# Router's sum over edges: the second one-hot of each step is made by TensorE transposes and a ScalarE copy instead of a VectorE comparison

## The reference, cut to what matters

```python
e = leaky_relu(a_src[src] + a_dst[dst], negative_slope=0.2)
e_max = segment_max(e, dst, num_segments=M)
ee = exp(e - e_max[dst])
denom = segment_sum(ee, dst, num_segments=M)
alpha = ee / (denom[dst] + 1e-16)
msg = h[src] * alpha[:, :, None]
agg = segment_sum(msg, dst, num_segments=M)
```

## Time and profile before

| | |
|---|---|
| median of three runs | 7634.4 us |
| the profiled execution, its own time | 7647.61 us |
| its span | 7645.7 us |
| busy, share of the span | PE 68%, PEld 54%, DVE 70%, ACT 34%, POOL 65% |
| mean granted TensorE clock | 0.75 of full speed |
| first and last `near_hot` of the router's sum | 7077.7 and 7475.6 us |
| first and last start of `add_up` | 7089.1 and 7493.1 us |

### The profile page before, as it was taken

One profiled execution on the slowest core, in us unless ns is written; L12 is line 12 of the kernel. 1 busy time (PEld: TensorE's weight loads), 2 busy tenths in 40 slices (PEclk: granted clock), 3 DMA queues, 4 the chain that ended last, 5 costly groups with the idle time before them and its releaser, 6 DMA issues. The chain is left out here.

```text
span 7645.7 us, 108407 instructions
## 1 busy us (share of the span) xinstructions
PE 5222.5 (68%) x27325; PEld 4150.9 (54%) x27325; DVE 5368.0 (70%) x15063; ACT 2576.8 (34%) x8277; POOL 4995.8 (65%) x5420
## 2 busy tenths in 40 slices
PE   6988766666666666566666666666669999998440
PEld 3655445555555555446556566556546666665340
DVE  8989746555555555667777777777757777777997
ACT  0000034444444444344444444444322222222220
POOL 2432317777777777557777777777247777776991
PEclk7555597878778778787878887887668888887555
DMA  1000234444444444344444444444333222322437
GB/s 32 4 8 4 47 103 134 135 134 135 133 135 133 133 134 135 107 122 131 131 130 131 131 131 131 131 131 131 113 62 63 59 62 59 63 58 55 126 92 181
DMA packets 504047, 777.31 MB, mean 102 GB/s; under 512 B 121545, under 2 KB 364222, under 8 KB 503442
## 3 DMA queue, kind: packets, MB, share of 16 engines
q0 software_dynamic: 202656, 454.22, 22.6%
q1 hardware_dynamic: 292838, 304.95, 15.0%
q10 hardware_dynamic: 7948, 11.21, 0.6%
HBM read 698.60 MB, written 71.36 MB: 101 GB/s over the span
## 5 line engine op out<-in xcount | busy, mean ns | idle before, releaser
L695 POOL DMA_INDIRECT att_kv_e<-kv,gnn_idx x3336 | 3195.4, 958 | 1193.6 <-issue 978.9
L771 PE MATMUL att_ps_sum<-att_vals,att_hot 128*125 128x136 f32 x6672 | 1301.7, 353 | 1537.9 <-DVE att_vals L825 1537.2
L771 PEld LDWEIGHTS att_ps_sum<-att_vals,att_hot 128*125 128x125 f32 x6672 | 1098.6, 239 | 1744.2 <-DVE att_vals L825 1735.9
L806 DVE TENSOR_TENSOR att_prod<-att_ps_q,att_kv_e 128x512 f32<-128x512 f32 x834 | 576.2, 691 | 1314.6 <-DMA att_kv_e<-kv,gnn_idx 797.1
L695 POOL DMA_INDIRECT max_rows<-rows,gat_idx x1128 | 1068.2, 947 | 564.8 <-issue 336.4
L758 PE MATMUL att_ps_q<-qs,att_hot_t 125*128 x6672 | 1195.9, 339 | 27.4 <-DVE att_hot_t L813 27.4
L758 PEld LDWEIGHTS att_ps_q<-qs,att_hot_t 125*128 125x128 f32 x6672 | 1142.5, 256 | 28.6 <-issue 28.6
L789 ACT ACTIVATE att_hot<-node_no,gnn_loc 128x125 f32<-128x125 f32 x3336 | 1044.3, 384 | 8.2 <-PEq L85 8.2
L1859 DVE CUSTOM_DVE_ANT_0 max_junk<-max_far,max_ps_b 125x256 bf16<-125x256 bf16 x2256 | 793.0, 416 | 259.4 <-PE max_ps_b L1823 258.4
L782 ACT ACTIVATE att_ps_dve<-att_clipped 128x32 f32<-128x32 f32 x834 | 167.7, 201 | 2310.9 <-DVE att_clipped L833 2310.5
L841 DVE TENSOR_TENSOR acc<-acc,att_ps_sum 125x136 f32 x1668 | 486.3, 292 | 125.2 <-DVE acc L841 12.0
(11 more groups left out here) (447 smaller groups left out, 7492.3 us busy)
## 6 DMA issues: line engine op xcount, KB each, us to landing
att_local<-gnn_loc_rows SPq DMA_DIRECT2D x834, 128.0 KB
att_kv_e<-kv,gnn_idx POOLq DMA_INDIRECT x3336, 3.0
max_local<-gat_loc_rows SPq DMA_DIRECT2D x282, 128.0 KB
gs_local<-gat_loc_rows SPq DMA_DIRECT2D x141, 256.0 KB, 3.2
outs<-ex_y SPq DMA_DIRECT2D x25, 896.0 KB
max_rows<-rows,gat_idx POOLq DMA_INDIRECT x1128, 2.4
ans_late<-outs SPq DMA_DIRECT2D x11, 896.0 KB
ans_early<-outs SPq DMA_DIRECT2D x8, 896.0 KB
```

Of the source, the lines that this page charges most:

```text
L695: pool.indirect_dma_start(rows(j, e), None, source, bass.IndirectOffsetOnAxis(ap=g.idx[:, t:t + 1], axis=0))\
L771: ins = pe.matmul(ps_sum[j % 2][0:NODE_TILE, p * 256:p * 256 + SUMS], hot[:, j, PAIR * p + e, :], vals[:, j % 2, PAIR * p + e, :], start=e ...
L806: dve.tensor_tensor(prod[:].rearrange("p (e d) -> p e d", e=GROUP), ps_q[j % 2][:, :].rearrange("p (e d) -> p e d", e=GROUP), kv_e[:, j, : ...
```

## The change

`one_hot` goes from VectorE, and `node_no` and its filling with it. In its place TensorE gets a piece `turn_hots` with lag -1 at the end of its list: eight transposes of `hot_t` (each 125 by 128, by way of the identity) into one of two PSUM tiles `ps_hot`, after `fetch` of two steps later. ScalarE gets a piece `copy_hots` with lag -2 at the end of its list, which copies 1000 columns from PSUM into `hot`. `hot_t` now has four buffers, and `near_hot` waits for the transposes of four steps earlier instead of the fetch of two steps earlier.

```diff
-        node_no = sb("node_no", [LANES, WIDE, NODE_TILE], BF16)
-        hot_t = sb("hot_t", [NODE_TILE, 2, WIDE * LANES], BF16)
+        hot_t = sb("hot_t", [NODE_TILE, 4, WIDE * LANES], BF16)
+        ps_hot = [st.enter_context(nc.psum_tensor(f"gs_ps_hot{h}", [LANES, 1024], BF16)) for h in range(2)]
...
-                                        hot_t[:, j % 2, e * LANES:(e + 1) * LANES],
+                                        hot_t[:, k % 4, e * LANES:(e + 1) * LANES],
...
+            def turn_hots(k, r, j):
+                wait(pe, m["one_hots"], k - 1)
+                for e in range(WIDE):
+                    ins = pe.transpose(ps_hot[j % 2][:, e * LANES:e * LANES + NODE_TILE],
+                                       hot_t[:, k % 4, e * LANES:(e + 1) * LANES], c.ident16[0:NODE_TILE, 0:NODE_TILE])
+                ins.then_inc(m["turned"], 1)
...
-            steps(pe, [(1, load_tiles), (-5, add_up), (1, fetch)])
+            steps(pe, [(1, load_tiles), (-5, add_up), (1, fetch), (-1, turn_hots)])
...
-            steps(act, [(-3, high), (-4, middle), (-1, exps)])
+            def copy_hots(k, r, j):
+                act.wait_ge(m["turned"], k + 1)
+                wait(act, m["summed"], (k - 4) + 1)
+                act.copy(hot[:, k % 4], ps_hot[j % 2][:].rearrange("p (e n) -> p e n", e=WIDE)[:, :, 0:NODE_TILE])\
+                    .then_inc(m["one_hots"], 1)
+            steps(act, [(-3, high), (-4, middle), (-1, exps), (-2, copy_hots)])
...
-            dve.memset(acc3[:], 0.0)
-            chain(dve.tensor_copy(node_no[:], c.node_no[:, 0:1, :].broadcast_to([LANES, WIDE, NODE_TILE])))
+            chain(dve.memset(acc3[:], 0.0))
...
-            def one_hot(k, r, j):
-                wait(dve, m["summed"], (k - 4) + 1)
-                dve.tensor_tensor(hot[:, k % 4], node_no[:], g.loc[:, bass.ds(k * WIDE, WIDE)].unsqueeze(2)
-                                  .broadcast_to([LANES, WIDE, NODE_TILE]), ALU.is_equal).then_inc(m["one_hots"], 1)
...
-                wait(dve, m["fetched"], k - 1)
-                dve.tensor_scalar(hot_t[:, j % 2, :], local[0:NODE_TILE, j], c.lane_no[0:NODE_TILE, :], None, ALU.is_equal)\
+                wait(dve, m["turned"], (k - 4) + 1)
+                dve.tensor_scalar(hot_t[:, k % 4, :], local[0:NODE_TILE, j], c.lane_no[0:NODE_TILE, :], None, ALU.is_equal)\
...
             steps(dve, [(0, gather_info), (-6, add_sum(0)), (-1, leaky), (-6, add_sum(1)), (2, near_hot), (-6, add_sum(2)),
-                        (-2, one_hot), (-6, add_sum(3)), (-6, load_tiles)])
+                        (-6, add_sum(3)), (-6, load_tiles)])
```

More of the change, by code:

```diff
@@ L1937, in neighbour_sum @@
         ps_n, ps_sum = psum("ps_n"), psum("ps_sum")
-        m = sem_set(nc, st, "gs", ["tiles_in", "cleared", "one_hots", "near_hots", "fetched", "info", "sums", "leaky",
+        ps_hot = [st.enter_context(nc.psum_tensor(f"gs_ps_hot{h}", [LANES, 1024], BF16)) for h in range(2)]
+        m = sem_set(nc, st, "gs", ["tiles_in", "cleared", "turned", "one_hots", "near_hots", "fetched", "info", "sums", "leaky",
                                    "less", "exps", "weighted", "high", "rest", "middle", "split", "summed", "added",
```

## The result

The changed kernel takes 7553.3 us (median of four runs, 7550.7 to 7561.8) where the kernel before takes 7634.1: a ratio of 0.9897, 95% interval 0.9879 to 0.9914, or 81 us less. The prediction was 7528 us in a range of 7495 to 7573. So the direction and the range hold, and of the 106 us forecast a quarter is missing; the time lies 3 us above the 7506 to 7550 to which the prediction gave 60%. The profiled execution takes 7550.7 us with a span of 7548.8.

The account below looks back on a forecast made before the run. VectorE and GpSimd were taken as the bound, fully busy at 2.905 us a step. VectorE's 2.10 plus 0.05 gives 2.15; 136 steps save 103 us, the ends 4, so 7528 us, range 7495 to 7573.

Parts of the forecast that it names:

- VectorE's 2.10 us: VectorE's time per step of the router's sum: 2.91 us, less the comparison's 1.11, plus 0.30 for the exposed add wait.
- their 0.43: On VectorE, the third and fourth add, now adjacent, would start 0.43 us apart, since one waits for the other.
- the 0.05 for handovers: Added to VectorE's 2.10 us because four engines hand work to each other, making 2.15 us a step.
- One of the prediction's own signs of being wrong: Signs: ScalarE's copy over 1.3 us, transposes over 0.15 us apart, or a step paced by a wait it did not name.
- the costly handovers: Rival, 18%: VectorE's waits for GpSimd or unhidden TensorE weight loads give 2.45 us a step, 7569 us.
- the 0.89 forecast: TensorE's eight new transposes of 125 columns per step take 0.89 us at 1.2 GHz, between 0.46 and 1.28.
- The rival that rested on serial transposes: Rival, 4%: each TensorE transpose starts only when the last has ended, eight take 2.18 us, 7693 us, slower.
- TensorE's idle time: Sign: TensorE's wait before its sums falls from 1.75 us a step to almost nothing.
- it gets out of step in the good way: Rival, 15%: GpSimd has gaps, VectorE waits less, TensorE is granted 2.4 GHz; 1.93 us a step, 7497 us.
- The loads of `local` were no bound here: Rival, 3%: nothing is gained because loads of `local` become the bound, at 119 GB/s; about 7634 us.
- it costs nothing: SyncE's 256 KB load lands 3.2 us after issue and is issued about four steps, 8.4 us, ahead.
- The ends: Start and finish of the router's sum, outside the 136 steps, would give 4 us, between 0 and 8.

Follow-up runs that it names:

- the run three deep: The changed kernel with hot_t three deep instead of four, near_hot waiting for the transposes of three steps earlier: 7720.9 us.
- run in halves: Changed kernel reading four tile numbers each step, near_hot cut into two halves of 512 columns, ahead of the third and fourth add: 7536.3 us.
- the run with four numbers: Changed kernel with the tile-number read moved behind near_hot and reading four numbers every step instead of eight every second: 7537.0 us.

## Why the prediction came out as it did

**VectorE's 2.10 us** was right in size: 2.03 us from gather to gather in a step without a read. The two adjacent adds are 0.41 us apart, as their 0.43 said. The waits inside moved: `leaky` takes 0.18 us instead of 0.52, and it no longer starts 0.03 us behind GpSimd's L1975 but just ahead of L1985; `near_hot` takes 0.74 instead of 0.64, with L1968 starting 0.05 us behind it, where it took 0.49 with no GpSimd instruction beside it (the run three deep, at 7252.47). That these neighbours are the cause is read from the rows.

**The step that failed** is the sum of VectorE itself, "2.91 - 1.11 + 0.30 = 2.10 us". It took the comparison as covering one thing, the wait between two adds. It covered a second: VectorE's read of tile numbers, 0.59 us every second step, which stands as the last piece of the list that the text before the prediction quotes. With it a step takes 2.67 us from gather to gather (7249.56 to 7252.23) instead of 2.03, which is 0.32 us a step in the mean, or 136 x 0.32 = 44 us, and gives the 2.35 that were measured. Only 136 x (2.353 - 2.15) = 28 us of them are missing from the forecast, because its 2.10 and the 0.05 for handovers stood 0.12 us above the 2.03 that VectorE needs without the read: the two errors partly cancelled. The read never showed as idle time before, so no row that I read named it; the list did. That the read is the cause is shown by moving it: 20.7 us of the stage came back.

**One of the prediction's own signs of being wrong came.** It named a step paced by a wait that stands in none of its lines, and VectorE's 0.52 us "for issue" before the gather is such a wait. The step of 2.353 us lies outside its 2.05 to 2.3. That the time is still within the range owes something to luck: the range reaches up to 7573 for the sake of the costly handovers, which did not come.

**The "0.05 us" for handovers** was beside the matter: with a read of four numbers most steps take 2.07 us, and the rest of the mean of 2.141 is in single longer steps, over half of it waits for loads of `local`.

**TensorE** was mis-sized a little and beside the path: a transpose lasts 0.310 us and the next starts about 0.10 behind it, so eight take 0.8 us instead of the 0.89 forecast.

```profile
L2017 PE MATMUL gs_ps_hot<-ident,gs_hot_t x1128: 267/310/314, 7066.3 to 7393.2; 125*128 125x125 bf16 x188
```

The page *TensorE: Matmul & The Clock Gate* of the Trainium skill, with 275 ns each, describes such a duration, not a spacing: eight in a row do not take 2.2 us here. The rival that rested on serial transposes fell with it. TensorE's idle time did not shrink to nothing as forecast; it is 0.22 and 0.79 us in turn.

**ScalarE**: the copy takes 0.973 us against 0.93.

```profile
L2052 ACT COPY gs_hot<-gs_ps_hot x141: 972/973/992, 7067.7 to 7393.6; 128x1000 bf16<-128x1000 bf16 x141
```

ScalarE's 1.86 us are hidden, shown by leaving copy and transposes out (2.340 against 2.353 us a step).

**GpSimd**: `less` takes 0.25 us instead of 1.27, as forecast; it now has gaps, which it gets from waiting for VectorE.

**The rivals**: "it gets out of step in the good way" needed the higher clock, which did not come. "The handovers cost more" came nearest in time (7569 against 7553), by a mechanism that is not there: `near_hot` grew by 0.10 us and `leaky` shrank by 0.34. The loads of `local` were no bound here: VectorE does not wait for one between 7100 and 7350 us. But "it costs nothing" holds at this pace only; at 2.2 us a step and below, VectorE waits for them behind most of the answer's loads (3.5 to 9.7 us in that stretch).

**The ends** of the stage gave 4.1 us where 4 was forecast, and the gain stayed a gain behind the stage: 79.2 us in the stage, 81 in the medians.

## What to carry to other kernels

When an instruction leaves a busy engine, list everything that engine's queue does while it runs: here a register read and a wait for a semaphore cost nothing under a comparison of 1.19 us and full price without it. Check this in the program's order as well as in the idle times, since covered work has no row of idle time. Work moved to engines with room is free only as deep as the buffers between them: with one buffer less the same change is slower than no change. And loads that were issued early enough have to be looked at again when the step gets shorter, with their slowest landing and not their median.

## What the runs showed of the hardware

- TensorE's granted clock stayed at 0.50, 1.2 GHz, with TensorE busy 88% (plain matmuls or transposes) and 95% (run in halves) of 250 us, while the stage of the router's maximum had 0.83 at 96%. In the run with weights and outputs 128 columns wide it was 0.58 in the mean, 0.50 from 7120 to 7200 us and 0.84 from 7260 to 7270, though TensorE was busy for only 79%. So here the higher clock did not go with the higher busy share; what moved it was not tried.
- The Trainium skill, in *TensorE: Matmul & The Clock Gate*, Part 4, says that transposes do not count for the clock; here transposes and matmuls by the identity give the same 0.50, so these runs cannot show that rule at work.
- A read of eight numbers into registers takes 0.59 to 0.60 us, of four 0.346, and holds up the queue of its engine.
- A load of 256 KB landed 3.3 us after its issue in the median of the run with four numbers, and after 6.8 to 8.3 us just behind the answer's loads (issues of 7118.3 to 7119.6 and of 7188.6 to 7191.3), with the DMA engines busy for 0.89 and 0.91 of those stretches (7115 to 7125 and 7185 to 7195 us) against 0.42 later (7220 to 7350 us).
- With the read of numbers moved within VectorE's list of the kernel before, the comparison blocks another GpSimd instruction, and the stage of 141 steps is 21.5 us longer.
